# Twelve of fifteen blocks of path comparisons in an alignment kernel: subtraction on GpSimd, one compare on VectorE

## The chip, the cores and the metric

The kernel runs on one core of one Trainium2 chip. The metric is the device time of that core in microseconds (us), the median of several runs. The engines are called PE (TensorE), DVE (VectorE), ACT (ScalarE), POOL (GpSimd) and SP (SyncE, which here only issues DMAs).

## The reference

A batch of 8 sequences of 56 tokens, 128 wide, goes through two gated layers, each an attention-like part and a feed-forward part. The change lies in the first part, an alignment by dynamic time warping of the normalized tokens ("large") with 1500 context rows ("small"):

```python
D = _pairwise_euclidean(small, large)            # 1500 x 56
R = _dtw_cost(D)      # R[i,j] = D[i,j] + min(R[i-1,j], R[i,j-1], R[i-1,j-1])
i_idx, j_idx, valid = _backtrack(R, T_small, T_large)   # argmin of diagonal, up, left, from the far corner
contrib = small[i_idx] * valid[:, None]
expanded = zeros((T_large, d)).at[j_idx].add(contrib)
x = x + tanh(g_xattn[0]) * alignment(ctx_1024, layernorm(x))
```

Then come a product-key memory layer (8 heads, 32 keys, gathers from tables), 16-head attention over the 1500 context rows of each batch (its keys are `ctx @ Wk + bk`), and a layer of 8 experts with the two best taken.

## The kernel before, in words

The cost matrix R is laid out by lanes. Each batch has 16 lanes (partitions); a lane holds 100 context rows at a time (C = 100; 15 stripes of 100 make 1500). The matrix is swept along a skewed front in STEPS = 70 steps of one column each. The R buffer holds one slot of 101 floats per step (SLOT).

**A step** on DVE (the loop `for t in range(STEPS)`, lines 1201 to 1231) is: a minimum of two shifted views of R's slot into `mring` (L1208, TENSOR_TENSOR), a shuffle that hands the last element of a lane to the next (L1209), a wait for the distances of that step, and a scan that adds distances and takes minima (L1213, TENSOR_TENSOR_SCAN), which raises `s_scan`. `mring` has 10 slots, so step t overwrites what step t-10 wrote.

**Blocks.** Steps are grouped in 14 blocks of TB = 5. To walk the path back later, each cell needs a "jump code". For a block k, `jump_inputs(k)` makes two marks per cell on DVE: `left` (L1189: is R's next element smaller than this one) and `never` (L1190: is the new R smaller than the minimum in `mring`). Both are `is_lt` of two float32 tensors, 128x500, with float16 results. It runs at step 9 for block 0, at step 5k+6 for blocks 1 to 12, and at step 68 and after the last step for the halves of the last block. Then PE's `jump_codes(k)` (L1387, L1389, L1391: three matmuls into one PSUM bank) adds them up, and DVE's `jump_targets(k)` (L1198, a scan over 505 elements, from PSUM) turns them into targets, at step 5k+14.

**Beside it.** For each block ACT copies the lane distances (L625, `lane_distances`, one block ahead of use) and works on key pieces of the second layer's attention: 32 pieces of 375 columns, each split in three bfloat16 parts by three ACT copies (L634, L640 twice) between which PE takes the rounded part off (L1370). `KEYS_OF_CHUNK` says how many pieces PE and ACT do in each block: 0, 1, then seven times 3, then five times 2. PE issues `jump_codes(k-2)` in chunk k, after the first key piece of that chunk. In the first 9 steps DVE also makes squared distances of 12 units, `d2_of(u)` (L849, from PSUM), placed by `D2_AT` before steps 1, 3, 5 and 8; units 8, 9 and 10 all stand before step 5. Each one is turned by PE (L1316), goes through a square root on ACT (L611) and is turned back into lane order (L1356). POOL does nothing between 24 us and 125 us.

**After it** come 69 hops back along the path (L1244 on DVE, L1452 on PE), the sums, and the other layers, one behind the other.

SP waits for `s_nv` of all 15 blocks before it loads the folding weights and the rest of the context.

Of the kernel before, what the change touches and what calls it, by code (L numbers as in the profile page):

```python
# [22 lines left out]
def view(ap, dims, offset=0):  # L23

    return bass.AP(tensor=ap.tensor, offset=ap.offset + offset, ap=[list(ap.ap[0])] + dims)


def build_gated_layers(nc, x_T, ctx_T, ctx_nat, g_xattn, g_ffn, weights, fold_w, w_tab, W1, W2, out):
# [5 lines left out]
    C = 100  # L34
# [39 lines left out]
    KPB = NI // KPIECE  # L74
    NKP = NB * KPB
    KBANKS = (4, 5, 6, 7)
    KEYS_OF_CHUNK = [0, 1] + 7 * [3] + 5 * [2]
    KEY_STEPS = [range(sum(KEYS_OF_CHUNK[:k]), sum(KEYS_OF_CHUNK[:k + 1])) for k in range(NTB)]
    assert KPIECE * KPB == NI and KRING == len(KBANKS) and NKP == sum(KEYS_OF_CHUNK)

# [15 lines left out]
    PAIR_BANK = (0, 1, 6)  # L96
    JOBS = [(i, lo, hi) for lo, hi in ((0, CUT), (CUT, TOK)) for i in range(FC)] + [(i, 0, TOK) for i in range(FC, NE * FC)]
    MORE = len(JOBS) - NE * FC
    CODES = [(k * TB, TB) for k in range(NTB - 1)] + [(STEPS - TB, TB - 1), (STEPS - 1, 1)]
    NCODES = len(CODES)  # L100
    TILES = (range(3), range(3, 4))
# [2 lines left out]
    with ExitStack() as ctx:  # L104
# [3 lines left out]
        def sem(name):  # L108
            return ctx.enter_context(nc.semaphore(name))
# [34 lines left out]

        mring = work[:, 0:2 * N_B]
        dts = work[:, 2 * N_B:4 * N_B]
        left = [work[:, 6 * N_B + a * N_B // 2:6 * N_B + (a + 1) * N_B // 2].bitcast(F16) for a in range(2)]
        o_nv = 8 * N_B + KQW
        never = [w.bitcast(F16) for w in (work[:, 7 * N_B + N_B // 2:8 * N_B], work[:, o_nv:o_nv + N_B // 2])]
        assert o_nv + N_B // 2 <= 10 * N_B  # L150
        gate = work[:, 10 * N_B:]
        taken = 0

# [275 lines left out]
        def _(sp):  # L429
# [10 lines left out]
            for n in range(NKP):  # L440
                store_keys(n)
                if n in (4, 10):
                    b = 1 + n // 10
                    sp.wait_ge(s_turn, UN)
                    sp.dma_start(nat[b], ctx_nat[:, b, :, :].rearrange("c s d -> c (s d)")).then_inc(s_nat2[b], 16)
            sp.wait_ge(s_nv, NCODES)
            sp.dma_start(foldw, fold_w[:, :]).then_inc(s_wqT, 16)
            for b in (0, *range(3, NB)):
                if b >= 3:
# [41 lines left out]
        def _(pool):  # L491
# [35 lines left out]
            pool.wait_ge(s_t, 2)  # L527
            done2(nc.gpsimd.tensor_tensor(mk[:, 1:2], mk2[:, :], mk[:, 0:1], ALU.subtract))
            done2(nc.gpsimd.tensor_scalar(mku[:, :], mk2[:, :], -1.0, 1.0, ALU.mult, ALU.add))
            pool.wait_ge(s_dt, NTB)  # L530
            for r in range(STORES):
                pool.wait_ge(s_kd[r], 16 * len(range(r, NKP, STORES)))
# [285 lines left out]
        def _(ve):  # L818
# [24 lines left out]
            def d2_of(u):  # L843

                ve.wait_ge(s_dot, u + 1)
                if u >= D_RING:
                    ve.wait_ge(s_turn, u - D_RING + 1)
                g = u % PAIRS
                nc.vector.tensor_scalar(sd[:, u % D_RING, :], ps[4 + u % 2][:, 0:PIECE], bbc[:, g:g + 1], 0.0,  # L849
                                        ALU.add, ALU.max).then_inc(s_d2, 1)  # L850
# [330 lines left out]

            shift = [LB - 1] + list(range(LB - 1)) + [2 * LB - 1] + list(range(LB, 2 * LB - 1))

            three = lambda a: a.rearrange("p (t c) -> p t c", c=C)

            def jump_inputs(k):

                t, n = CODES[k]
                nc.vector.tensor_tensor(three(left_of(k)), R_slot(t, n, 1, C), R_slot(t, n, 0, C), ALU.is_lt)  # L1189
                nc.vector.tensor_tensor(three(never_of(k)), R_slot(t + 1, n, 0, C),  # L1190
                                        three(mring[:, t % (2 * TB) * C:(t % (2 * TB) + n) * C]), ALU.is_lt
                                        ).then_inc(s_nv, 1)

            def jump_targets(k):

# [2 lines left out]
                nc.vector.tensor_tensor_scan(where[:, t * SLOT:(t + n) * SLOT], gate[:, 0:n * SLOT],  # L1198
                                             ps[3 - k % 2][:, 0:n * SLOT], 0.0, ALU.add, ALU.max).then_inc(s_carry, 1)

            D2_AT = {1: (6,), 3: (7,), 5: (8, 9, 10), 8: (11,)}
            for t in range(STEPS):
                for u in D2_AT.get(t, ()):
                    d2_of(u)
                m = mring[:, (t % (2 * TB)) * C:(t % (2 * TB) + 1) * C]
                if t >= 1:
                    ve.wait_ge(s_scan, t)
                nc.vector.tensor_tensor(m, R_slot(t, 1, 1, C), R_slot(t, 1, 0, C), ALU.min)  # L1208
                link(nc.vector.stream_shuffle(R_slot(t + 1, 1, 0, 1), R_slot(t, 1, C, 1), shift))  # L1209
                if t % DT_STEPS == 0:  # L1210
                    ve.wait_ge(s_dtc, t // DT_STEPS + 1)
                d = dts[:, (t % (2 * DT_STEPS)) * C:(t % (2 * DT_STEPS) + 1) * C]
                nc.vector.tensor_tensor_scan(view(R, [[1, C]], (t + 1) * SLOT + 1), m, d,  # L1213
                                             R[:, (t + 1) * SLOT:(t + 1) * SLOT + 1], ALU.min, ALU.add
                                             ).then_inc(s_scan, 1)
                if t == 2 * TB - 1:
                    ve.wait_ge(s_scan, t + 1)
                    jump_inputs(0)
                    link(nc.vector.tensor_scalar(lane_i[:, :], pidx[:, :], DH, None, ALU.bitwise_and))
                    nc.vector.tensor_scalar(rowc21[:, :], rowc2[:, :], 1.0, None, ALU.add)  # L1220
                    link(nc.vector.tensor_copy(hm[:, 0:1], lane_i[:, :]))
                    link(nc.vector.tensor_scalar(hm[:, 1:2], hm[:, 0:1], 0.0, None, ALU.is_gt))
                    link(nc.vector.tensor_scalar(hm[:, 0:1], hm[:, 1:2], 0.0, None, ALU.is_equal))
                if t % TB == 1 and t >= 2 * TB:
                    jump_inputs(t // TB - 1)
                if t == STEPS - 2:
                    ve.wait_ge(s_scan, t + 1)
                    ve.wait_ge(s_code, NTB - 2)
                    jump_inputs(NTB - 1)
                if t % TB == 4 and t >= 2 * TB:  # L1230
                    jump_targets(t // TB - 2)
            ve.wait_ge(s_scan, STEPS)
            jump_inputs(NTB)
            for k in range(NTB - 2, NCODES):
                jump_targets(k)

# [43 lines left out]
        def _(pe):  # L1280
# [98 lines left out]
                    take_off(n - 1, 1)  # L1379

            def jump_codes(k):
                pe.wait_ge(s_nv, k + 1)
                if k >= 2:
                    pe.wait_ge(s_carry, k - 1)
                bank, n = ps[3 - k % 2], CODES[k][1]
                inner = view(bank, [[SLOT, n], [1, C]], 1)
                nc.tensor.matmul(bank[:, 0:n * SLOT], one16[:, :], steps16[:, 0:n * SLOT], start=True, stop=False,  # L1387
                                 skip_group_check=True)
                nc.tensor.matmul(inner, one16[:, :], left_of(k), start=False, stop=False,  # L1389
                                 skip_group_check=True)  # L1390
                nc.tensor.matmul(inner, never16[:, :], never_of(k), start=False, stop=True,  # L1391
                                 skip_group_check=True).then_inc(s_code, 1)
# [407 lines left out]
```

## Time and profile before

| | |
|---|---|
| median of 3 runs | 517.43 us (517.33 to 517.56) |
| the profiled execution | 516.99 us, of which the span from first to last instruction 515.2 us |
| granted TensorE clock, mean | 0.946 |
| DVE busy | 372.8 us (72%) |
| PE busy | 422.9 us (82%) |
| ACT, POOL busy | 255.2 us (50%), 64.7 us (13%) |
| steps 0 to 69 | scans from 26.4 us to 118.1 us of the span |

A timeline row gives the start in us, the duration in us, the engine, the line of the kernel, the operation, what it writes and reads, partitions x elements with types, and how many instructions are merged in the row. In square brackets stands how long the engine was idle before it and who released it. A DVE instruction may start a little before the one in front has ended, so costs are best taken from start to start.

### The profile page before, as it was taken

Reading aid. Unit: us, or ns where it says so; the run is one execution under the profiler, and the core shown is the slowest. Engines: PE = TensorE matmul, PEld = TensorE weight load, DVE = VectorE, ACT = ScalarE, POOL = GpSimd, SP = SyncE. Lnnn points to the kernel's source line nnn. Section 1 sums busy time; section 2 is a strip of 40 time slices with the busy share of each in tenths; the row PEclk is TensorE's granted clock in tenths of the full one; section 3 lists DMA queues with packets and bytes.
Section 4 is the critical chain, followed back from the end, with each engine's and each line's share of the span. In section 5 each row is a group of like instructions: output and inputs, shape, how many; then the busy total and the mean of one; then the engine's idle time right before and its main releaser. Section 6 shows DMA issues by size and latency. Waiting matters only on the chain.

```text
span 515.2 us, 10127 instructions
## 1 busy us (share of the span) xinstructions
PE 422.9 (82%) x4013; PEld 253.2 (49%) x4013; DVE 372.8 (72%) x979; ACT 255.2 (50%) x442; POOL 64.7 (13%) x99
## 2 busy tenths in 40 slices
PE   8998877677888888200788899999999999989996
PEld 5444433345555574000334456666666666654443
DVE  7659999997666794865686898888888884462222
ACT  4665877553322591100102456665666567655443
POOL 1000000001000001677430000210210210200000
PEclk9999999888999999655789999999999999999999
DMA  8600764334422103893162004383483582000000
GB/s 283 241 0 25 213 198 144 102 125 122 153 60 80 41 3 67 204 240 90 56 135 50 1 1 101 84 180 86 98 180 74 111 269 62 1 1 1 0 1 18
DMA packets 28941, 50.28 MB, mean 98 GB/s; under 512 B 2470, under 2 KB 18622, under 8 KB 28894
## 3 DMA queue, kind: packets, MB, share of 16 engines
q1 hardware_dynamic: 27070, 45.96, 33.0%
q0 software_dynamic: 1536, 3.67, 2.9%
q8 instruction: 32, 0.52, 0.5%
q14 instruction: 15, 0.12, 0.1%
q10 hardware_dynamic: 288, 0.00, 0.0%
HBM read 39.96 MB, written 9.45 MB: 96 GB/s over the span
## 4 chain that ended last, share of the span: by engine, by line
PE 47%; DVE 35%; issue 7%; POOL 6%; ACT 2%; DMA 1%; DVEq 0%
PE banks L1608 7%; PE banks L1584 7%; POOL arena L554 6%; PE banks L1639 5%; DVE arena L1213 5%; PE banks L1681 5%; DVE work L1244 5%; DVE mx L1019 4%; PE banks L1696 4%; DVE arena L1268 2%; PE banks L1452 2%; DVE work L1208 2%; DVE mx L1027 2%; PE banks L1301 2%; PE banks L1323 2%
## 5 line engine op out<-in xcount | busy, mean ns | idle before, releaser
L1019 DVE TENSOR_REDUCE mx<-banks 112x1 f32<-112x500 f32 x168 | 107.1, 675 | 16.4 <-PE banks L1584 16.4
L762 ACT ACTIVATE arena<-banks 128x896 f32<-128x896 f32 x96 | 87.9, 917 | 48.3 <-PE banks L1639 47.7
L1323 PE MATMUL banks<-steps,one 128*128 128x500 f16 (+1 forms) x188 | 53.8, 380 | 32.9 <-DVE hcol L967 32.9
L1608 PE MATMUL banks<-arena 128*32 128x112 f32 (+1 forms) x1536 | 57.1, 265 | 1.5 <-ACT arena L762 0.9
L1584 PE MATMUL banks<-ctxT,arena 96*112 96x500 bf16 x144 | 54.7, 393 | 3.8 <-DVE mx L1019 1.1
L1608 PEld LDWEIGHTS banks<-arena 128*32 128x32 f32 (+1 forms) x1536 | 33.6, 109 | 21.5 <-issue 18.9
L1244 DVE SCALAR_TENSOR_TENSOR work<-twice,banks,arena 128x202 f32<-128x202 f32 x68 | 29.5, 434 | 18.7 <-PE banks L1452 18.7
L1639 PEld LDWEIGHTS banks<-arena,ctxT 99*128 99x128 bf16 (+1 forms) x576 | 37.5, 103 | 10.2 <-issue 2.4
L1323 PEld LDWEIGHTS banks<-steps,one 128*128 128x128 f16 x188 | 19.2, 104 | 47.1 <-issue 37.4
L1639 PE MATMUL banks<-arena,ctxT 99*128 99x112 bf16 (+1 forms) x576 | 41.2, 213 | 0.3 <-issue 0.3
L640 ACT ACTIVATE arena<-banks,wts 128x375 bf16<-128x375 f32 x64 | 33.9, 597 | 7.5 <-PE banks L1370 7.5
L554 POOL DMA_INDIRECT arena<-in_w_tab,idx x32 | 34.3, 1071 | 17.9 <-issue 9.4
L1400 PE MATMUL banks<-wts,ctxT 128*128 128x128 f32 x192 | 34.8, 283 | 0.0
L775 ACT ACTIVATE arena<-banks,wts 128x448 f32<-128x448 f32 (+2 forms) x36 | 21.3, 592 | 25.0 <-PE banks L1681 24.7
L1213 DVE TENSOR_TENSOR_SCAN arena<-work,arena 128x100 f32<-128x100 f32 x70 | 29.8, 426 | 4.3 <-ACT work L625 1.8
L1400 PEld LDWEIGHTS banks<-wts,ctxT 128*128 128x128 f32 x192 | 32.4, 197 | 0.5 <-issue 0.2
L1370 PE MATMUL banks<-arena,minusb 128*128 128x375 bf16 x64 | 19.1, 342 | 15.8 <-ACT arena L634 14.4
L1681 PE MATMUL banks<-xnT,arena 128*128 128x448 f32 (+2 forms) x72 | 31.1, 514 | 0.0
L671 ACT ACTIVATE arena<-banks 128x512 f32<-128x512 f32 (+2 forms) x32 | 14.2, 492 | 33.3 <-PE banks L1400 31.4
L1363 PE MATMUL banks<-ctxT,wts 128*128 128x375 f32 x64 | 27.4, 514 | 0.0
L1584 PEld LDWEIGHTS banks<-ctxT,arena 96*112 96x112 bf16 x144 | 18.1, 128 | 17.5 <-issue 9.5
L1696 PE MATMUL banks<-arena 128*128 128x448 f32 (+2 forms) x64 | 26.5, 496 | 0.0
(269 smaller groups left out, 697.7 us busy)
## 6 DMA issues: line engine op xcount, KB each, us to landing
ctxT<-key_parts SPq DMA_DIRECT2D x36, 375.0 KB, 6.7
key_parts<-arena SPq DMA_DIRECT2D x32, 281.2 KB, 3.1
ctxT<-in_ctx_T SPq DMA_DIRECT2D x12, 500.0 KB, 9.0
arena<-key_parts SPq DMA_DIRECT2D x12, 375.0 KB, 7.8
ctxT<-in_ctx_nat SPq DMA_DIRECT2D x5, 750.0 KB
arena<-in_ctx_nat SPq DMA_DIRECT2D x3, 750.0 KB
arena<-in_L_ffn_W SPq DMA_DIRECT2D x1, 2048.0 KB, 9.7
arena<-in_fold_w SPq DMA_DIRECT2D x1, 768.0 KB, 6.0
```

Of the source, the lines that this page charges most:

```text
L554: nc.gpsimd.indirect_dma_start(out=gath[:, t, h, :], out_offset=None, in_=w_tab[:, :], in_offset=bass.IndirectOffsetOnAxis(ap=idx[:, c:c + ...
L762: nc.scalar.activation(Pt[0:rows, g % 2, :].rearrange("p (a n) -> p a n", a=2), banks[0:rows, 2 + 2 * (g % 2):4 + 2 * (g % 2), 0:HQ // 2], ...
L1019: nc.vector.tensor_reduce(mx3[:, b % 2, u // NPIECE, u % NPIECE:u % NPIECE + 1], ps[k % 2][0:2 * NJ, 0:PIECE], AX_X, ALU.max).then_inc(s_m ...
L1213: nc.vector.tensor_tensor_scan(view(R, [[1, C]], (t + 1) * SLOT + 1), m, d, R[:, (t + 1) * SLOT:(t + 1) * SLOT + 1], ALU.min, ALU.add).the ...
L1244: nc.vector.scalar_tensor_tensor(out=hit_at.rearrange("p (c k) -> p c k", k=2), in0=twice[:, :].rearrange("p (c k) -> p c k", k=2), scalar ...
L1323: nc.tensor.matmul(bank[:, 0:cols], one16[:, :], steps16[:, 0:cols], start=True, stop=True, skip_group_check=True)
L1400: last = nc.tensor.matmul(ps[VALUE_BANKS[n % 6]][0:rows, k * D:(k + 1) * D], ctxT[:, b * NI + c * P:b * NI + c * P + rows], Wv_sb, start=T ...
L1584: nc.tensor.matmul(ps[k % ring][0:2 * NJ, 0:PIECE], QP[0:NPR, u // NPIECE, b, :], KP[b % 3][0:NPR, u // NPIECE, (u % NPIECE) * PIECE:(u % ...
L1608: last = nc.tensor.matmul(ps[6 + b % 2][q:q + 32, o:o + 2 * NJ], vals[0:rows, v0:v0 + 32], Pt[0:rows, g % 2, 2 * t * NJ:2 * (t + 1) * NJ], ...
L1639: last = nc.tensor.matmul(bank[0:rows, o:o + 2 * NJ], KP[b % 3][0:NPR + 3, m, c * P:c * P + rows], QP[0:NPR + 3, m, b, :], start=True, sto ...
L1681: nc.tensor.matmul(ps[5 + j % 2][:, lo:hi], W1s[:, e, c * P:(c + 1) * P], xnT[:, lo:hi], start=True, stop=True, skip_group_check=True).the ...
L1696: nc.tensor.matmul(ps[7 if e % 2 else 0][:, lo:hi], W2s[:, i, :], hT[:, i % 4, lo:hi], start=(c == 0), stop=(c == FC - 1), skip_group_chec ...
```

## The change

It takes the two compares of blocks 0 to 11 off DVE. POOL subtracts instead (two TENSOR_TENSOR of 128x500 elements per block, float32 in, bfloat16 out, both results side by side in a `gaps` buffer), and DVE makes both marks with one TENSOR_SCALAR `is_lt 0` over 1000 bfloat16 elements, float16 out (`signs_of`), after the scan of step 5k+10. POOL starts block k when the scan of step 5k+4 is done. DVE waits for POOL's block before a step that would overwrite `mring` (at steps 10, 15, ...). Blocks 12, 13 and 14 keep the two compares (`moves_of`), at the places they had. The key pieces are dealt out in another order, five small table instructions move from behind step 9 to in between units 8 and 9, and unit 10 moves from before step 5 to before step 6.

```diff
-    KEYS_OF_CHUNK = [0, 1] + 7 * [3] + 5 * [2]
+    KEYS_OF_CHUNK = [0, 1] + [3, 2, 3, 3, 2, 3, 2, 3, 3, 2, 3, 2]
+    SIDE = NTB - 2
-        left = [work[:, 6 * N_B + a * N_B // 2:6 * N_B + (a + 1) * N_B // 2].bitcast(F16) for a in range(2)]
-        never = [w.bitcast(F16) for w in (work[:, 7 * N_B + N_B // 2:8 * N_B], work[:, o_nv:o_nv + N_B // 2])]
+        moves = [work[:, (6 + a) * N_B:(7 + a) * N_B].bitcast(F16) for a in range(2)]
+        left = [m[:, 0:N_B] for m in moves]
+        never = [m[:, N_B:2 * N_B] for m in moves]
+        gaps = [work[:, (4 + a) * N_B:(5 + a) * N_B].bitcast(BF16) for a in range(2)]
@@ SP
-            sp.wait_ge(s_nv, NCODES)
+            sp.wait_ge(s_nv, SIDE)
+            sp.wait_ge(s_nvl, NCODES - SIDE)
@@ POOL
+            for k in range(SIDE):
+                pool.wait_ge(s_scan, CODES[k][0] + TB)
+                if k >= 2:
+                    pool.wait_ge(s_nv, k - 1)
+                t, n = CODES[k]
+                nc.gpsimd.tensor_tensor(three(gaps[k % 2][:, 0:N_B]), R_slot(t, n, 1, C), R_slot(t, n, 0, C), ALU.subtract)
+                nc.gpsimd.tensor_tensor(three(gaps[k % 2][:, N_B:2 * N_B]), R_slot(t + 1, n, 0, C),
+                                        three(mring[:, t % (2 * TB) * C:(t % (2 * TB) + n) * C]), ALU.subtract
+                                        ).then_inc(s_gap, 1)
@@ DVE
-            def jump_inputs(k):
+            def moves_of(k):
...
-                                        ).then_inc(s_nv, 1)
+                                        ).then_inc(s_nvl, 1)
+            def signs_of(k):
+                ve.wait_ge(s_gap, k + 1)
+                if k >= 2:
+                    ve.wait_ge(s_code, k - 1)
+                nc.vector.tensor_scalar(moves[k % 2][:, :], gaps[k % 2][:, :], 0.0, None, ALU.is_lt).then_inc(s_nv, 1)
...
-            D2_AT = {1: (6,), 3: (7,), 5: (8, 9, 10), 8: (11,)}
+            D2_AT = {1: (6,), 3: (7,), 5: (8, 9), 6: (10,), 8: (11,)}
             for t in range(STEPS):
                 for u in D2_AT.get(t, ()):
                     d2_of(u)
+                    if u == 8:
+                        spare_tables()
...
+                if t % TB == 0 and t >= 2 * TB:
+                    ve.wait_ge(s_gap, min(t // TB - 1, SIDE))
...
-                if t == 2 * TB - 1:
-                    ve.wait_ge(s_scan, t + 1)
-                    jump_inputs(0)
...
-                if t % TB == 1 and t >= 2 * TB:
-                    jump_inputs(t // TB - 1)
+                if t % TB == 0 and 2 * TB <= t < (SIDE + 2) * TB:
+                    signs_of(t // TB - 2)
+                if t == SIDE * TB + TB + 1:
+                    ve.wait_ge(s_code, SIDE - 1)
+                    moves_of(SIDE)
@@ PE
-                pe.wait_ge(s_nv, k + 1)
+                pe.wait_ge(s_nv if k < SIDE else s_nvl, k + 1 if k < SIDE else k + 1 - SIDE)
```

## Rows read from the trace of the kernel before

**Rows 1.** The page: the chain that ended last, shares of the span.
```profile
PE 47%; DVE 35%; issue 7%; POOL 6%; ACT 2%; DMA 1%; DVEq 0%
```

**Rows 2.** Windows: length, then PE, PEld, DVE, ACT, POOL busy, clock, DMA share, GB/s.
```profile
50.00:75.00 25.00, 20.30 (x89) 10.38 (x88) 23.88 (x93) 20.14 (x44) 0.00 (x0) 1.00 0.70 214
```

**Rows 3.** Timeline of DVE, one block, from one jump_targets to the next.
```profile
73.97 0.43 DVE L1213 TENSOR_TENSOR_SCAN arena<-work,arena 128x100 f32<-128x100 f32 x1
74.32 1.18 DVE L1198 TENSOR_TENSOR_SCAN arena<-work,banks 128x505 f16<-128x505 f32 x1
75.41 0.24 DVE L1208 TENSOR_TENSOR work<-arena 128x100 f32<-128x100 f32 x1
...
76.22 0.26 DVE L1208 TENSOR_TENSOR work<-arena 128x100 f32<-128x100 f32 x1
...
76.94 0.65 DVE L1189 TENSOR_TENSOR work<-arena 128x500 f16<-128x500 f32 x1
77.51 0.67 DVE L1190 TENSOR_TENSOR work<-arena,work 128x500 f16<-128x500 f32 x1
78.10 0.26 DVE L1208 TENSOR_TENSOR work<-arena 128x100 f32<-128x100 f32 x1
...
78.93 0.27 DVE L1208 TENSOR_TENSOR work<-arena 128x100 f32<-128x100 f32 x1
...
80.49 1.18 DVE L1198 TENSOR_TENSOR_SCAN arena<-work,banks 128x505 f16<-128x505 f32 x1
```

**Rows 4.** Groups by line and form: DVE's shuffle of one column, a cast of 896 elements.
```profile
L1209 DVE STREAM_SHUFFLE arena<-arena 128x1 f32<-128x1 f32 x70 | 10.6, 151 | 0.0
...
L1005 DVE CAST work<-arena 128x896 bf16<-128x896 f32 x1 | 0.6, 628 | 0.0
```

**Rows 5.** Groups by line and form: POOL's TENSOR_TENSOR with two full inputs.
```profile
L585 POOL TENSOR_TENSOR work<-work 128x224 f32<-128x224 f32 x7 | 4.6, 660 | 0.6
...
L590 POOL TENSOR_TENSOR work<-work 128x112 f32<-128x112 f32 x7 | 3.0, 423 | 26.7 <-DVE work L1051 26.7
```

**Rows 6.** Timelines of POOL and of DVE where both run at 261 us.
```profile
261.36 1.09 POOL L565 TENSOR_SCALAR_AFFINE_SELECT work<-work 24x1024 bf16<-24x1024 bf16 x1
...
261.66 0.27 DVE L904 TENSOR_TENSOR xc<-xT,banks 128x112 f32<-128x112 f32 x1 [0.66 <-PE banks L1283]
261.96 0.62 DVE L905 TENSOR_TENSOR xsq<-xc 128x112 f32<-128x112 f32 x1
```

**Rows 7.** The same at 442 us, and POOL's line 591: ns min/median/max.
```profile
441.84 0.57 DVE L1102 SCALAR_TENSOR_TENSOR xT<-xc,gt,xT 128x336 f32<-128x336 f32 x1
...
442.00 0.64 POOL L591 TENSOR_TENSOR work<-work,wts 128x112 f32<-128x112 f32 x1
...
L591 POOL TENSOR_TENSOR work<-work,wts x7: 374/375/640, 329.6 to 442.0; 128x112 f32<-128x112 f32 x7
```

**Rows 8.** Timelines of DVE, ACT and PE around steps 5 to 10.
```profile
34.16 0.74 DVE L849 TENSOR_SCALAR arena<-banks,bbc 128x500 f32<-128x500 f32 x1 [1.77 <-PE banks L1305]
37.23 0.74 DVE L849 TENSOR_SCALAR arena<-banks,bbc 128x500 f32<-128x500 f32 x1 [2.34 <-PE banks L1305]
...
43.73 0.15 DVE L1219 TENSOR_SCALAR lane_i<-pidx 128x1 int32<-128x1 int32 x1
...
44.56 0.26 DVE L1208 TENSOR_TENSOR work<-arena 128x100 f32<-128x100 f32 x1
...
44.93 0.42 DVE L1213 TENSOR_TENSOR_SCAN arena<-work,arena 128x100 f32<-128x100 f32 x1
...
41.03 0.75 PE L1316 MATMUL banks<-ident,arena 128*100 128x128 f32 x5 [0.65 <-DVE arena L849]
...
43.56 0.59 ACT L625 ACTIVATE work<-banks 128x500 f32<-128x500 f32 x1 [1.09 <-PE banks L1356]
```

**Rows 9.** Timelines of PE and ACT in a block with three key pieces.
```profile
76.23 0.38 PE L1387 MATMUL banks<-steps,one 128*128 128x505 f16 x1
...
80.67 0.59 ACT L625 ACTIVATE work<-banks 128x500 f32<-128x500 f32 x1 [1.40 <-DVE arena L1213]
```

More of the change, by code:

```diff
@@ L146, in build_gated_layers @@
         dts = work[:, 2 * N_B:4 * N_B]
-        left = [work[:, 6 * N_B + a * N_B // 2:6 * N_B + (a + 1) * N_B // 2].bitcast(F16) for a in range(2)]
-        o_nv = 8 * N_B + KQW
-        never = [w.bitcast(F16) for w in (work[:, 7 * N_B + N_B // 2:8 * N_B], work[:, o_nv:o_nv + N_B // 2])]
-        assert o_nv + N_B // 2 <= 10 * N_B
+        moves = [work[:, (6 + a) * N_B:(7 + a) * N_B].bitcast(F16) for a in range(2)]
+        left = [m[:, 0:N_B] for m in moves]
+        never = [m[:, N_B:2 * N_B] for m in moves]
+        gaps = [work[:, (4 + a) * N_B:(5 + a) * N_B].bitcast(BF16) for a in range(2)]
         gate = work[:, 10 * N_B:]
@@ L328, in build_gated_layers @@
         s_scan = sem("column_scanned")
+        s_gap = sem("moves_compared")
+        s_nvl = sem("last_not_left_marks_ready")
         s_nv = sem("rows_not_left_ready")
@@ L422, in left_of @@
             return left_last[:, :] if k == NCODES - 1 else left[k % 2][:, 0:CODES[k][1] * C]
+        three = lambda a: a.rearrange("p (t c) -> p t c", c=C)
         R_slot = lambda k, n, lo, cnt: view(R[:, :], [[SLOT, n], [1, cnt]], k * SLOT + lo)
@@ L1182, in _ @@
             shift = [LB - 1] + list(range(LB - 1)) + [2 * LB - 1] + list(range(LB, 2 * LB - 1))
-            three = lambda a: a.rearrange("p (t c) -> p t c", c=C)
-            def jump_inputs(k):
+            def moves_of(k):
                 t, n = CODES[k]
@@ L1199, in jump_targets, with spare_tables @@
                                              ps[3 - k % 2][:, 0:n * SLOT], 0.0, ALU.add, ALU.max).then_inc(s_carry, 1)
-            D2_AT = {1: (6,), 3: (7,), 5: (8, 9, 10), 8: (11,)}
+            def spare_tables():
+                link(nc.vector.tensor_scalar(lane_i[:, :], pidx[:, :], DH, None, ALU.bitwise_and))
+                nc.vector.tensor_scalar(rowc21[:, :], rowc2[:, :], 1.0, None, ALU.add)
+                link(nc.vector.tensor_copy(hm[:, 0:1], lane_i[:, :]))
+                link(nc.vector.tensor_scalar(hm[:, 1:2], hm[:, 0:1], 0.0, None, ALU.is_gt))
+                link(nc.vector.tensor_scalar(hm[:, 0:1], hm[:, 1:2], 0.0, None, ALU.is_equal))
+            D2_AT = {1: (6,), 3: (7,), 5: (8, 9), 6: (10,), 8: (11,)}
             for t in range(STEPS):
@@ L1215, in _ @@
                                              ).then_inc(s_scan, 1)
-                if t == 2 * TB - 1:
-                    ve.wait_ge(s_scan, t + 1)
-                    jump_inputs(0)
[L1219 to L1223, printed above, removed]
-                if t % TB == 1 and t >= 2 * TB:
-                    jump_inputs(t // TB - 1)
+                if t % TB == 0 and 2 * TB <= t < (SIDE + 2) * TB:
[3 more added lines that the diff above has]
+                    moves_of(SIDE)
                 if t == STEPS - 2:
@@ L1228, in _ @@
                     ve.wait_ge(s_code, NTB - 2)
-                    jump_inputs(NTB - 1)
+                    moves_of(NTB - 1)
                 if t % TB == 4 and t >= 2 * TB:
@@ L1232, in _ @@
             ve.wait_ge(s_scan, STEPS)
-            jump_inputs(NTB)
+            moves_of(NTB)
             for k in range(NTB - 2, NCODES):
```

## The prediction

> **What bounds the kernel now.** I read the chain first [rows 1]: PE and DVE share it, so the kernel is a row of stages, each with its own limit, and a change counts only in its stage. The change lies in steps 0 to 69, before 122 us. The windows say what limits there [rows 2]: between 50 and 75 us DVE is busy for 23.88 of 25.00 us, ACT for 20.14, POOL not at all. The timeline of one block [rows 3] says the same in detail: DVE runs from one jump_targets (74.32) to the next (80.49), 6.17 us, without an idle gap that another engine ended. After step 69 the hops follow at once, and they wait for DVE's last targets. So a microsecond that DVE gains or loses in steps 10 to 69 is one of the whole kernel, as long as DVE stays the limit.
>
> **One block taken apart** [rows 3]. A plain step takes 0.83 us (78.10 to 78.93; over several steps 0.84). The step with the two compares takes 1.88 us (76.22 to 78.10), so the pair costs 1.04. The step scan at 73.97 is over at 74.40; call this T. The next minimum would start 0.03 later, and starts at 75.41 because of jump_targets: 0.98. Sum: 5 x 0.84 + 1.04 + 0.98 = 6.2, which is the 6.17 seen.
>
> **Removed.** Blocks 0 to 11 lose the pair: 1.04 us each.
>
> **Added on DVE: the compare with zero.** No row shows a single-source instruction with 16-bit input in SBUF. A cast of 896 float32 elements takes 0.63 us, about 0.15 of it fixed (a shuffle of one column takes 0.15) [rows 4]. At that rate per element, 1000 elements take 0.15 + 0.53 = 0.68; at that rate per byte read (2000 bytes against 3584) 0.15 + 0.27 = 0.42. At no rate can it be under 0.15. The cast reads and writes nearly as many bytes as fit, so I take 0.42. It starts 0.08 before the scan in front has ended (80.49 against 80.57 [rows 3]) and the next minimum then follows 0.08 before its end, where a minimum otherwise starts 0.03 after the scan: 0.42 - 0.08 - 0.08 - 0.03 = 0.23 net. The ends are 0 and 0.50.
> The Trainium skill ("VectorE: DVE Perf Modes", the perf-mode tier table) gives 693 ns for 2048 bfloat16 elements of a tensor_scalar, four per cycle; an estimate from it is 0.41 us here. The sum would stay as it is.
>
> **Moved to POOL: two subtractions a block.** POOL's TENSOR_TENSOR with two full inputs takes 0.423 us for 112 elements and 0.660 for 224 [rows 5], so 2.12 ns an element and 0.19 fixed: 1.25 us for 500. Two take 2.5 us in a block of about 6, so POOL is no limit by its own time. The results are used five steps later, and `mring` is overwritten five steps later, so DVE's new wait for POOL costs 0.
>
> **What it costs on DVE is another thing.** While POOL ran an instruction from 261.36 to 262.45, DVE's L904, which has one input in PSUM, took its plain 0.27 us. L905, the same size with both inputs in SBUF, started at 261.96 and took 0.62: it was held until POOL had ended, and was done 0.13 later [rows 6]. At 442 us it is the other way round: DVE's L1102 ran to 442.41, and POOL's L591 took 0.64 where its median is 0.375, done 0.23 after DVE [rows 7]. So a DVE instruction with two SBUF inputs and a POOL instruction that reads SBUF don't run together here; the second one waits for the whole of the first.
> The Trainium skill ("SBUF — State Buffer", who interferes with whom) has this as a rule: the shared port pair is an exclusive lock, and the second to issue is blocked for the whole instruction. Both places in this trace agree with it. By a reader who took the ports as free, the sum would come out faster; that is the first rival below.
>
> DVE's minimum (L1208) and step scan (L1213) both have two SBUF inputs; jump_targets has one in PSUM and is free of this. One block then runs so. POOL starts at T + 0.08 and ends its first subtraction at T + 1.33. DVE is in jump_targets until then; its minimum is issued at T + 1.01 and held to T + 1.33, done at T + 1.45. The shuffle has one input. The second subtraction reads on from T + 1.45 for 1.06 us, to T + 2.52. The scan is issued at T + 1.56, held, and done some 0.25 after POOL, at T + 2.77. In the trace it is done 0.03 before the minimum at 76.22 [rows 3], T + 1.79. Cost: 0.98 us a block. If POOL keeps the ports between its two instructions, the minimum is held as well, to T + 2.6, and the scan ends at T + 3.16: 1.37. Rows 6 show DVE let in at POOL's end, but POOL's next one waited for a semaphore there. I take 1.1, nearer to the row. The ends are 0 (no collision) and 1.7 (POOL at 1.4 us each, and keeping the ports). When the compare with zero comes, POOL is done.
>
> So a block changes by -1.04 + 0.23 + 1.10 = +0.29. There are ten such (the steps 15 to 64): **+2.9 us**.
>
> **Front.** Unit 9 waits 1.77 us and unit 10 waits 2.34 [rows 8]. The five table instructions (43.73 to 44.56, 0.83) move into the first wait, step 5 (0.84) into the second; both are hidden, and if POOL's first block holds some of them, the wait still covers it. Units 11, its turn and its lane distances follow PE, not DVE alone: PE waited 0.65 for DVE at 41.03, so L625 at 43.56 comes 0.6 earlier, done at 43.55, and the scan of step 10 (before: 44.93 to 45.35) can't start sooner. But block 1's subtractions start at 42.2, are held by one minimum, and end at 44.6; the scan then ends at 44.85. So 0.5 is won there; block 1's pair goes (1.04), one compare with zero comes (0.23): **-1.3 us**. Without a collision it is 2.2.
>
> **End.** Block 11's compare stands at step 65, its pair is already counted: **+0.2**. Blocks 12 to 14 are as before.
>
> **Key pieces: 0.** In a three-piece block ACT idles 1.40 us before the next lane distances [rows 9]. PE gets to the jump codes at T + 1.83 (76.23) and will now wait for the compare, done at T + 3.1, so 1.3 later, with one more key piece behind it. That fits into the 1.40 and the longer block, and a two-piece block gives slack back; the distances are made a block ahead. POOL's and SP's queues hold nothing that is due before step 69.
>
> **Sum:** 2.9 - 1.3 + 0.2 = +1.8 us. The profiled execution took 516.99 us, 0.44 below the median; it would be 518.8, and the median 517.43 + 1.8 = **519.2 us**. In this case's own bounds (0.8 to 1.4 for the collision, 0.23 to 0.5 for the compare) it lies between 515.7 and 524.
>
> **Rivals.**
> *The ports don't collide for these instructions* (POOL's reads yield, or its lock is short). Then a block changes by -0.81: 10 x -0.81 - 2.2 + 0.2 = -10.1, about 507.3 us. Rows 6 and 7 speak against it; they show two events, one of another POOL operation. It decides the sign: below 0.81 us of collision a block the ten blocks gain, and half a collision gives 512. Chance 0.20.
> *The compare takes one or two elements a cycle, not four.* 0.68 us, 0.50 net: 12 x 0.27 = 3.2 more, 522.4 us. That the change doesn't do what it says would be this. Chance 0.08.
> *PE and ACT become the limit* in the seven three-piece blocks, since PE's jump codes wait for the compare. If the compare ends later than T + 3.1, ACT's slack is gone; 0.3 us in seven blocks is 2 more, 521 us. Against it: slack from one block carries to the next. Chance 0.06.
>
> **Chances.** About 0.2% (1.03 us) is what a measurement of this kernel can tell from no change. My forecast's case has 0.66: with +1.8 in its middle and bounds on both sides of zero, 0.38 slower, 0.18 within, 0.10 faster. Rival one is 0.20 faster. The other two give 0.12 slower, of which 0.02 within. Together: faster 0.30, same 0.20, slower 0.50. The range reaches from 510 (half of the first rival's ground) to 524.
>
> **What would show it.** In the changed trace: POOL's subtractions near 1.25 us; the step scan or minimum right behind jump_targets taking 1 us or more where it took 0.43 and 0.26, and ending just behind a POOL instruction; the compare at 0.42 us; a block at about 6.5 us from one jump_targets to the next, against 6.17. The forecast is wrong if those two stay at 0.43 and 0.26 (then blocks are near 5.4 us), if the compare is near 0.7, or if DVE shows idle time before jump_targets that PE ended.

## The result, and the profile after

The changed kernel takes 514.16 us in the median of 7 runs (513.17 to 515.97), the kernel before 517.46 on the same chip; the ratio is 0.994, 95% interval 0.9921 to 0.9959. That is 3.3 us faster. One of the seven runs of the kernel before took 678.99 us and is left out of the ratio; the other six took 516.38 to 517.68. Forecast was 519.2, slower by 1.8, with 0.30 for faster. The profiled execution took 514.87 us, with a span of 513.1.

The page after, its chain [rows 1]; then the windows [rows 2]:

```profile
PE 47%; DVE 31%; issue 10%; POOL 7%; ACT 2%; DMA 2%; DVEq 0%; POOLq 0%
```
```profile
50.00:75.00 25.00, 19.04 (x84) 9.68 (x82) 23.88 (x89) 19.36 (x41) 9.60 (x9) 1.00 0.64 189
```

DVE is busy for the same 23.88 of 25 us, but with fewer instructions. Part of that "busy" is now waiting inside an instruction. The timeline of DVE shows it, one block from jump_targets (now L1219) to jump_targets [rows 3]; L1240 is the minimum, L1245 the step scan, L1213 the compare with zero:

```profile
72.26 0.42 DVE L1245 TENSOR_TENSOR_SCAN arena<-work,arena 128x100 f32<-128x100 f32 x1
72.60 1.18 DVE L1219 TENSOR_TENSOR_SCAN arena<-work,banks 128x505 f16<-128x505 f32 x1
73.70 0.23 DVE L1240 TENSOR_TENSOR work<-arena 128x100 f32<-128x100 f32 x1
...
74.05 1.11 DVE L1245 TENSOR_TENSOR_SCAN arena<-work,arena 128x100 f32<-128x100 f32 x1
75.08 0.39 DVE L1213 TENSOR_SCALAR work<-work 128x1000 f16<-128x1000 bf16 x1
75.39 0.25 DVE L1240 TENSOR_TENSOR work<-arena 128x100 f32<-128x100 f32 x1
...
78.59 1.18 DVE L1219 TENSOR_TENSOR_SCAN arena<-work,banks 128x505 f16<-128x505 f32 x1
```

The timeline of POOL in the same stretch, and its two lines grouped over all twelve blocks (compare [rows 5]):

```profile
72.76 1.02 POOL L541 TENSOR_TENSOR work<-arena 128x500 bf16<-128x500 f32 x1 [3.83 <-DVE arena L1245]
73.74 1.19 POOL L542 TENSOR_TENSOR work<-arena,work 128x500 bf16<-128x500 f32 x1
```
```profile
L542 POOL TENSOR_TENSOR work<-arena,work 128x500 bf16<-128x500 f32 x12 | 14.4, 1200 | 0.0
L541 POOL TENSOR_TENSOR work<-arena 128x500 bf16<-128x500 f32 x12 | 12.3, 1025 | 54.5 <-DVE arena L1245 54.5
```

The step scan behind jump_targets takes 1.11 us instead of 0.43 and ends at 75.16, 0.23 behind POOL's second subtraction (74.93). A block takes 5.99 us (72.60 to 78.59) where it took 6.17. Eleven scans out of 70 are longer than 0.45 us: ten of 1.10 to 1.15, and that of step 10 with 0.77.

The front, in the timelines of DVE and ACT around steps 5 to 10 [rows 8] (L864 is units 9 and 10, L640 the lane distances):

```profile
34.80 0.74 DVE L864 TENSOR_SCALAR arena<-banks,bbc 128x500 f32<-128x500 f32 x1 [1.13 <-PE banks L1332]
37.56 0.42 DVE L1245 TENSOR_TENSOR_SCAN arena<-work,arena 128x100 f32<-128x100 f32 x1 [1.77 <-ACT work L640]
37.90 0.71 DVE L864 TENSOR_SCALAR arena<-banks,bbc 128x500 f32<-128x500 f32 x1
...
44.33 0.77 DVE L1245 TENSOR_TENSOR_SCAN arena<-work,arena 128x100 f32<-128x100 f32 x1 [1.35 <-ACT work L640]
```
```profile
43.65 0.59 ACT L640 ACTIVATE work<-banks 128x500 f32<-128x500 f32 x1 [1.10 <-PE banks L1383]
```

Where the time went, from the ends of the step scans in both traces (this execution began its steps 0.6 us later than the other, so stretches are compared, not times):

| stretch | before | after | difference | forecast |
|---|---|---|---|---|
| scan 4 to scan 14 | 18.32 | 16.62 | -1.70 | -1.3 |
| scan 14 to 64, ten blocks | 61.66 | 60.16 | -1.50 | +2.9 |
| scan 64 to 69 | 7.14 | 7.32 | +0.18 | +0.2 |
| sum | 87.12 | 84.10 | -3.02 | +1.8 |

The sum of -3.0 is the measured -3.3 within what runs differ by. Behind the last step the two traces are alike: the first hop starts 3.72 us after the last scan before, 3.71 after.

### The profile page after: what moved, and what is told of

Its sections match the earlier page's. It is cut to its first block, busy times and chain, and to the rows that moved or that the text cites. A ratio compares the mean times of both kernels' runs of the same rounds, so it can differ in the third digit from the quotient of the medians.

```text
span 513.1 us, 10171 instructions
## 1 busy us (share of the span) xinstructions
PE 422.1 (82%) x4013; PEld 252.1 (49%) x4013; DVE 369.7 (72%) x967; ACT 255.5 (50%) x442; POOL 91.3 (18%) x123
## 4 chain that ended last, share of the span: by engine, by line
PE 47%; DVE 31%; issue 10%; POOL 7%; ACT 2%; DMA 2%; DVEq 0%; POOLq 0%
PE banks L1635 7%; PE banks L1611 7%; POOL arena L569 7%; PE banks L1666 5%; PE banks L1708 5%; DVE work L1271 5%; DVE mx L1034 5%; PE banks L1723 4%; DVE arena L1245 4%; DVE arena L1295 2%; PE banks L1328 2%; DVE mx L1042 2%; PE banks L1479 2%; DVE work L1240 2%; PE banks L1332 2%
## 5 line engine op out<-in xcount | busy, mean ns | idle before, releaser
L1245 DVE TENSOR_TENSOR_SCAN arena<-work,arena 128x100 f32<-128x100 f32 x70 | 37.2, 531 | 7.3 <-ACT work L640 5.0
L1427 PE MATMUL banks<-wts,ctxT 128*128 128x128 f32 x192 | 33.2, 273 | 0.1
L1427 PEld LDWEIGHTS banks<-wts,ctxT 128*128 128x128 f32 x192 | 30.5, 186 | 0.6 <-ACT arena L686 0.3
L595 POOL TENSOR_TENSOR work<-arena,mk 128x448 f32<-128x448 f32 x7 | 6.5, 932 | 129.9 <-ACT arena L753 129.9
```

The costliest lines, as they stand in the source:

```text
L1427: last = nc.tensor.matmul(ps[VALUE_BANKS[n % 6]][0:rows, k * D:(k + 1) * D], ctxT[:, b * NI + c * P:b * NI + c * P + rows], Wv_sb, start=T ...
```

## The experiments

All are timed beside the kernel before on the same chip, 4 to 10 runs each but for the two of POOL's rates; the chip differs from experiment to experiment, so the ratios compare better than the times. "Block" is the distance of the ends of scans 14, 19, ... in the profiled execution.

### POOL writes, but does not read

```diff
+        spare = [work[:, (8 + a) * N_B:(9 + a) * N_B].bitcast(BF16) for a in range(2)]
...
-                nc.gpsimd.tensor_tensor(three(gaps[k % 2][:, 0:N_B]), R_slot(t, n, 1, C), ...)
-                nc.gpsimd.tensor_tensor(three(gaps[k % 2][:, N_B:2 * N_B]), ...).then_inc(s_gap, 1)
+                nc.gpsimd.memset(spare[k % 2], 0.0)                 # 1000 bfloat16, an unused place
+                nc.gpsimd.memset(gaps[k % 2][:, :], 0.0).then_inc(s_gap, 1)
```

> From the changed kernel; POOL's two subtractions a block become two memsets of 1000 bfloat16 elements each (about 0.9 us each by the memsets in the trace), so POOL works as long but reads nothing. The compare with zero then sees zeros, so the jump codes carry no path. Theory A (a DVE instruction with two SBUF inputs and a POOL instruction that reads SBUF exclude each other): no step scan is longer than 0.43 us, a block goes from 6.0 to about 5.3 us, the kernel to about 507 us. Theory B (any POOL work beside DVE holds it, by writes or by the queue): the scans behind jump_targets stay near 1.1 us, blocks near 6.0, the kernel near 514. Theory C (PE and ACT are the next limit close below): scans at 0.43, but DVE idle in the blocks and blocks over 5.5 us.

This kernel leaves the differences out, so the path that it follows means nothing; it makes the same steps, compares and hops. Measured: 507.33 us, ratio 0.9812 (0.9789 to 0.9835), blocks 5.34 to 5.35. The timelines of DVE and POOL:

```profile
76.00 0.23 DVE L1239 TENSOR_TENSOR work<-arena 128x100 f32<-128x100 f32 x1
...
76.35 0.43 DVE L1244 TENSOR_TENSOR_SCAN arena<-work,arena 128x100 f32<-128x100 f32 x1
76.69 0.43 DVE L1212 TENSOR_SCALAR work<-work 128x1000 f16<-128x1000 bf16 x1
```
```profile
75.92 0.93 POOL L543 MEMSET work<- 128x1000 bf16 x1
```

The scan at 76.35 runs beside POOL's memset (75.92 to 76.85) at its plain 0.43. So POOL's reads hold the two-input instructions, not its work as such, and the 0.67 us a block that this run gives back (6.01 to 5.34) is the price of the collision. Theory A holds, B falls. C did not show from scan 19 on; the two stretches before took 5.69 and 5.65. In the first of them step 10 waits for its distances, in the second DVE waits 0.22 for jump codes from PE. 507.3 is also what the first rival named, the case without a collision.

### The collision alone

```diff
@@ POOL, in the kernel before; jump_inputs unchanged
+            for k in range(SIDE):
+                pool.wait_ge(s_scan, CODES[k][0] + TB)
+                nc.gpsimd.tensor_tensor(...)
+                nc.gpsimd.tensor_tensor(...).then_inc(s_gap, 1)
@@ DVE
+                if t % TB == 0 and t >= 2 * TB:
+                    ve.wait_ge(s_gap, min(t // TB - 1, SIDE))
```

> From the kernel before; POOL makes the same two subtractions at the same points beside it, and nobody uses them; the float32 compares stay on DVE. This is the collision alone. Theory A: the step scan behind jump_targets grows from 0.43 to about 1.1 us, a block from 6.17 to 6.86, ten of them and the front together about 7.5 us, so about 525 us. Theory B' (the long scan of the changed kernel comes from the new order of waits, not from the ports): under 1 us more than before.

Measured: 527.06 us, ratio 1.0192 (1.0159 to 1.0225), blocks 6.83 to 6.89. DVE and POOL:

```profile
46.38 0.93 DVE L1231 TENSOR_SCALAR rowc<-rowc 100x15 f32<-100x15 f32 x1
...
81.77 1.11 DVE L1224 TENSOR_TENSOR_SCAN arena<-work,arena 128x100 f32<-128x100 f32 x1
```
```profile
45.71 1.57 POOL L538 TENSOR_TENSOR work<-arena,work 128x500 bf16<-128x500 f32 x1
...
81.46 1.20 POOL L538 TENSOR_TENSOR work<-arena,work 128x500 bf16<-128x500 f32 x1
```

The same scan grows by the same 0.69, a block from 6.17 to 6.86. The whole costs 9.9 us, not 7.5: the block of steps 10 to 14 takes 8.81 instead of 7.22, since POOL there meets the compares of block 0 (the second took 1.49 for 0.67) and the table instructions. One of these, with one float32 input of 15 columns, took 0.93 (0.17 in the changed kernel) and ended 0.03 behind POOL's second subtraction. From scan 4 to scan 69 that makes 8.6 us; the other 1.3 lie outside the steps, and no run here says why.

### POOL one step later

```diff
-                pool.wait_ge(s_scan, CODES[k][0] + TB)
+                pool.wait_ge(s_scan, CODES[k][0] + TB + 1)
```

> From the changed kernel; POOL starts each block one step later, after the scan of step 5k+5, so that jump_targets no longer runs beside its first subtraction. Theory A: both subtractions now meet only instructions with two SBUF inputs (and the compare with zero); about 1.0 us more is held a block, blocks near 7.0 us, the kernel near 524 us. If jump_targets gives no cover, blocks stay at 6.0 us and the kernel at 514.

Measured: 524.17 us, ratio 1.0141 (1.0115 to 1.0167), blocks 6.81 to 6.87. DVE and POOL:

```profile
86.12 1.08 DVE L1240 TENSOR_TENSOR work<-arena 128x100 f32<-128x100 f32 x1
...
87.31 1.15 DVE L1245 TENSOR_TENSOR_SCAN arena<-work,arena 128x100 f32<-128x100 f32 x1
```
```profile
85.97 1.11 POOL L541 TENSOR_TENSOR work<-arena 128x500 bf16<-128x500 f32 x1 [4.59 <-DVE arena L1245]
87.05 1.20 POOL L542 TENSOR_TENSOR work<-arena,work 128x500 bf16<-128x500 f32 x1
```

Now each of the two subtractions holds one instruction of DVE: 0.82 for the minimum (1.08 less 0.26) and 0.7 for the scan. Between them DVE was let in: the minimum ends at 87.20, 0.12 behind the end of the first subtraction (87.08), and the second one, already started at 87.05, takes 1.20. So POOL does not keep DVE out from one instruction to the next. That jump_targets covers the first subtraction is worth 0.83 us a block, 10 us in all; the place of POOL's start decides the sign of this change.

### What a subtraction costs on POOL

```diff
+            for _ in range(2):
+                for n in (112, 224, 336, 448):
+                    tried_one(xsq[:, 0:n], A0(0, n), A0(200, n))                          # inputs 0 and 200
+                tried_one(grid(xsq[:, :], 4, 56, 56), grid(wts[:, :], 4, 56, 112), grid(wts[:, 56:], 4, 56, 112))
+                tried_one(h16[:, 0:448], A0(0, 448), A0(200, 448))                        # h16: bfloat16 out
...
+                tried_one(grid(h16, 5, 100, 100), grid(wts[:, 1:], 5, 100, 101), grid(wts[:, :], 5, 100, 101))
+                tried_one(xsq[:, :], A0(0, 448), wts[:, 0:1].broadcast_to([P, 448]))
```

> From the changed kernel; 20 more POOL subtractions in a stretch of the attention where POOL is idle and DVE reads only PSUM, on scratch, each of the ten forms twice. It prices the term that the forecast had at 1.25 us and the trace has at 1.02. Theory A: 0.25 us fixed and 1.54 ns an element whatever the output type, so 112, 224, 336, 448 elements give 0.42, 0.60, 0.77, 0.94 us, and only the 4x56 form with stride 112 costs 0.66. Rival: the bfloat16 output is what is cheap, so float32 at 448 gives 1.14 and bfloat16 0.93.

These instructions stand in a stretch where POOL is otherwise idle, and each of the two kernels that hold them ran once (515.24 and 523.59 us); they are read for the durations alone. Measured, first round (the second agrees within 0.02): float32 out, both inputs plain rows 200 elements apart: 0.42, 0.66, 0.91 and 1.13 us for 112, 224, 336 and 448 elements. Four rows of 56, the inputs 56 apart: 0.66. bfloat16 out: 0.66, 1.13 and 1.26 for 224, 448 and 500 elements. Five rows of 100 at step 101, the inputs 1 apart: 1.01. One input a single repeated element, 448: 0.93. Two lines of POOL's timeline, the plain row of 500 and the five rows of 100:

```profile
298.76 1.26 POOL L593 TENSOR_TENSOR xsq<-wts 128x500 bf16<-128x500 f32 x1
...
300.83 1.01 POOL L593 TENSOR_TENSOR xsq<-wts 128x500 bf16<-128x500 f32 x1
```

Neither theory holds. The output type changes nothing (448 elements: 1.13 both ways), and the forecast's rate of 2.12 ns an element is right for plain rows. Yet the form of the kernel costs a fifth less.

```diff
+            for a, b in ((0, 200), (0, 201), (1, 201), (0, 1), (0, 0), (0, 101)):            # plain rows of 500
+                tried_one(grid(a, 1, 500, 500), grid(b, 1, 500, 500))
+            for a, b, s in ((0, 200, 100), (0, 1, 100), (1, 0, 101), (0, 0, 101), (0, 101, 101), (0, 101, 102), (0, 192, 101)):
+                tried_one(grid(a, 5, 100, s), grid(b, 5, 100, s), 5, 100)                     # 5 rows of 100 at step s
+            tried_one(grid(0, 1, 500, 500), grid(4, 1, 500, 500))
+            tried_one(grid(0, 1, 500, 500), grid(8, 1, 500, 500))
```

> From the changed kernel; 15 more POOL subtractions of 500 elements, bfloat16 out, on scratch where POOL is idle: plain rows at several starts, 5 rows of 100 at steps 100, 101 and 102. Before it, plain rows of 500 (starts 0 and 200) took 1.25 us and 5 rows of 100 at step 101 (starts 1 and 0) took 1.02. Theory P (how the starts of the two inputs stand to each other sets the rate): the pairs 0 and 1, 0 and 201, 0 and 101 take 1.02 in either shape, 0 and 200 take 1.25. Theory Q (short rows are faster): all forms of 5 rows take 1.02 and all plain ones 1.25.

Measured, in this order: 1.24, 1.07, 1.25, 1.02, 1.02, 1.07; then 1.25, 1.02, 1.02, 1.02, 1.06, 1.06, 1.25; then 1.02 and 1.25. Four of them, with the inputs 200, 1, 4 and 8 elements apart:

```profile
295.77 1.24 POOL L593 TENSOR_TENSOR xsq<-wts 128x500 bf16<-128x500 f32 x1 [33.10 <-DVE mx L1052]
...
299.56 1.02 POOL L593 TENSOR_TENSOR xsq<-wts 128x500 bf16<-128x500 f32 x1
...
311.15 1.02 POOL L593 TENSOR_TENSOR xsq<-wts 128x500 bf16<-128x500 f32 x1
...
312.25 1.25 POOL L593 TENSOR_TENSOR xsq<-wts 128x500 bf16<-128x500 f32 x1
```

Theory P holds, but for 0.05 at two of its distances, and Q falls: rows and steps don't matter, the distance between the two inputs does. Distances 0, 1 and 4 gave 1.02, 101 and 201 gave 1.06 to 1.07, and 8, 192 and 200 gave 1.25. In the kernel before, the two instructions that I priced by have their inputs 56 and 112 elements apart [rows 5], which are multiples of 8 like the slow ones here, and they cost what plain rows 200 apart cost (0.66 for 224 elements, 0.42 for 112). The kernel's first subtraction has them 1 apart. The fast distances were not tried at 112 or 224 elements.

### One subtraction only

```diff
@@ POOL
-                nc.gpsimd.tensor_tensor(three(gaps[k % 2][:, 0:N_B]), R_slot(t, n, 1, C), R_slot(t, n, 0, C), ALU.subtract)
@@ DVE, signs_of
-                nc.vector.tensor_scalar(moves[k % 2][:, :], gaps[k % 2][:, :], 0.0, None, ALU.is_lt).then_inc(s_nv, 1)
+                t, n = CODES[k]
+                nc.vector.tensor_tensor(three(left_of(k)), R_slot(t, n, 1, C), R_slot(t, n, 0, C), ALU.is_lt)
+                nc.vector.tensor_scalar(never[k % 2], gaps[k % 2][:, N_B:2 * N_B], 0.0, None, ALU.is_lt).then_inc(s_nv, 1)
```

> From the changed kernel; for blocks 0 to 11 POOL makes only the second subtraction (against the minimum), as its first and only one, and DVE makes the other mark itself with a float32 is_lt of 500 elements ahead of a compare with zero of 500 elements. Theory A: the one subtraction of about 1.0 us lies wholly beside jump_targets, so no scan is held (0.69 us a block back) and DVE pays about 0.57 for the float32 mark less 0.13 for the shorter compare. Blocks go from 6.0 to about 5.8 us, the kernel from 514.2 to about 511.8 us. If the collision were not what the second subtraction costs, this would only add 0.44 us a block: about 519 us.

Measured: 514.01 us, ratio 0.9926 (0.9907 to 0.9945), which can't be told from the changed kernel. Blocks 5.85 to 5.91. DVE and POOL:

```profile
73.07 0.32 DVE L1242 TENSOR_TENSOR work<-arena 128x100 f32<-128x100 f32 x1
...
73.50 0.43 DVE L1247 TENSOR_TENSOR_SCAN arena<-work,arena 128x100 f32<-128x100 f32 x1
73.84 0.65 DVE L1213 TENSOR_TENSOR work<-arena 128x500 f16<-128x500 f32 x1
74.42 0.28 DVE L1214 TENSOR_SCALAR work<-work 128x500 f16<-128x500 bf16 x1
```
```profile
72.14 1.13 POOL L541 TENSOR_TENSOR work<-arena,work 128x500 bf16<-128x500 f32 x1 [4.72 <-DVE arena L1247]
```

No scan is held, as expected. But this subtraction (R against the minimum) takes 1.13 to 1.18 us in the blocks (1.23 for the first of them) with no other subtraction before it, not 1.02, and so holds the minimum by 0.1. The block gains 0.13 instead of 0.25, and the last block loses 0.46, since block 11's float32 mark now also stands in it (7.78 against 7.32). The expectation of 511.8 us had left out both.

### Parts put back: the key deal and the front

```diff
-    KEYS_OF_CHUNK = [0, 1] + [3, 2, 3, 3, 2, 3, 2, 3, 3, 2, 3, 2]
+    KEYS_OF_CHUNK = [0, 1] + 7 * [3] + 5 * [2]
```

> From the changed kernel; only the deal of the key pieces is put back (seven times 3, then five times 2). Theory A (DVE is the limit, the deal is worth next to nothing): 514 to 515 us, early blocks at 6.0 or 6.1. Rival (the deal is what gained): about 517 us, with DVE idle in front of jump_targets in the blocks of three pieces.

Measured: 514.72 us, ratio 0.9938 (0.9923 to 0.9954). In its trace scan 4 to scan 69 takes 84.10 us, the same as in the changed kernel. The deal is worth nothing in this stage.

```diff
-            D2_AT = {1: (6,), 3: (7,), 5: (8, 9), 6: (10,), 8: (11,)}
+            D2_AT = {1: (6,), 3: (7,), 5: (8, 9, 10), 8: (11,)}
-                    if u == 8:
-                        spare_tables()
+                if t == 2 * TB - 1:
+                    spare_tables()
```

> From the changed kernel; only unit 10 and the five table instructions are put back where they were (before step 5, behind step 9). Theory A: step 10 waits for lane distances and for POOL anyway, so of the 1.67 us moved only about 0.5 comes back: 514.7 us. If the whole of it counts: 515.8 us.

Measured: 515.35 us, ratio 0.9954 (0.9937 to 0.9971). In the trace, scan 4 to scan 9 takes 11.09 us against 10.60, and all later stretches agree within 0.03: 0.5 us, as theory A has it. The medians differ by 1.2, but the intervals of the two ratios overlap.

### The type of the differences

```diff
-        moves = [work[:, (6 + a) * N_B:(7 + a) * N_B].bitcast(F16) for a in range(2)]
+        moves = [work[:, (8 + a) * N_B:(9 + a) * N_B].bitcast(F16) for a in range(2)]
...
-        gaps = [work[:, (4 + a) * N_B:(5 + a) * N_B].bitcast(BF16) for a in range(2)]
+        gaps = [work[:, (4 + 2 * a) * N_B:(6 + 2 * a) * N_B] for a in range(2)]      # float32
```

> From the changed kernel; POOL writes float32 differences, and DVE's compare reads 1000 float32 elements instead of bfloat16. Theory A: the compare goes from 0.39 to about 0.68 us (the rate of the float32 cast), 0.28 a block for twelve blocks, POOL's subtractions stay at 1.02 us: about 517.5 us. If the type makes POOL's instruction cheap, they grow towards 1.25 as well and a block loses 0.3 more: about 520 us.

Measured: 517.39 us, ratio 0.9995 (0.9981 to 1.0009), blocks 6.25 to 6.30. DVE's scan is as before, the compare grows:

```profile
74.95 1.11 DVE L1245 TENSOR_TENSOR_SCAN arena<-work,arena 128x100 f32<-128x100 f32 x1
75.98 0.65 DVE L1213 TENSOR_SCALAR work<-work 128x1000 f16<-128x1000 f32 x1
```

POOL's first subtraction stays at 1.02 us, so the type does not make it cheap. Bfloat16 is worth 0.26 us of DVE in each of twelve blocks, 3.1 us, which is about as much as the change gains: with float32 differences it is a draw with the kernel before.

### Distances read from PSUM

```diff
@@ DVE, the step
-                    ve.wait_ge(s_dtc, t // DT_STEPS + 1)
-                d = dts[:, (t % (2 * DT_STEPS)) * C:(t % (2 * DT_STEPS) + 1) * C]
+                    ve.wait_ge(s_dt, t // DT_STEPS + 1)
+                d = ps[t // DT_STEPS % 2][:, t % DT_STEPS * C:(t % DT_STEPS + 1) * C]
@@ PE, lane_columns (and no lane_distances on ACT)
-                    pe.wait_ge(s_dtc, q - 1)
+                    pe.wait_ge(s_scan, DT_STEPS * (q - 1))
@@ PE, the end: four value tiles wait for scan 65, eight stand behind jump_codes(NTB - 2) and scan 70
```

> From the changed kernel; the step scan reads the distances from the PSUM bank in which PE has turned them, and ACT's copy to SBUF is left out. PE now waits where ACT waited, and four value tiles come later, behind the last step. Theory A (it is the second SBUF input that a POOL read holds up): the scan behind jump_targets takes its plain 0.43 us while POOL's second subtraction runs, and the hold moves to the compare with zero, which reads SBUF alone but came out fast: 0.39 grows to about 0.9, blocks near 5.9 us. If any DVE read of SBUF were held, the scan would stay at 1.1.

Measured: 513.25 us, ratio 0.9894 (0.986 to 0.9929), blocks 5.72 to 5.76. DVE and POOL:

```profile
72.18 0.42 DVE L1241 TENSOR_TENSOR_SCAN arena<-work,arena,banks 128x100 f32<-128x100 f32 x1
72.52 0.83 DVE L1209 TENSOR_SCALAR work<-work 128x1000 f16<-128x1000 bf16 x1
...
117.46 1.34 DVE L1215 TENSOR_TENSOR_SCAN arena<-work,banks 128x404 f16<-128x404 f32 x2 [2.34 <-PE banks L1414]
```
```profile
71.88 1.19 POOL L542 TENSOR_TENSOR work<-arena,work 128x500 bf16<-128x500 f32 x1
```

The scan with one input in PSUM runs at 0.42 beside POOL's read, and the hold moves to the compare, which reads only one tensor but is held all the same (0.83 for 0.39). The block gains 0.27, and the step scan is no slower from PSUM. The last row shows what this version loses: behind the last step DVE waits 2.34 us for jump codes that stand behind value tiles on PE.

### A faster version

```diff
-    VALUE_BANKS = (0, 1, 4, 5, 6, 7)
-    EARLY_VALUES = 16
+    VALUE_BANKS = (0, 4, 1, 5, 6, 7)
+    EARLY_VALUES = 14
@@ PE, the end
+            jump_codes(NTB - 2)      # then value tiles 4 to 7
+            jump_codes(NTB - 1)      # then scan 70, tiles 8 to 10
+            jump_codes(NTB)          # then tiles 11 to 13
```

> From distances_in_psum; the end of the stage is put in order: the value tiles that have to wait for a bank now stand behind the jump codes that DVE waits for (the second group in bank 4, the third in bank 1, two early tiles fewer). DVE idled 2.34 us there, behind the last step. Theory A: that comes back, blocks stay at 5.74 us, the kernel goes from 513.2 to about 511 us. If the gain of the blocks is lost elsewhere: 513.

Measured: 511.4 us, ratio 0.9895 (0.9873 to 0.9918), blocks 5.73 to 5.76. The first hop follows the last scan after 3.71 us again, where it was 6.26. The ratios of this version and the one before it (0.9894) can't be told apart, so this gain too rests on the traces.

```diff
-                if t % TB == 0 and 2 * TB <= t < (SIDE + 2) * TB:
+                if t % TB == 1 and 2 * TB <= t < (SIDE + 2) * TB:
                     signs_of(t // TB - 2)
```

> From psum_tail; the compare with zero moves one step later, behind the scan of step 5k+11. Theory A: POOL's second subtraction has then ended when the compare comes (0.39 again), but it holds the minimum of that step, which reads twice from SBUF, by about 0.3 us where it held the compare by 0.43. Blocks about 5.6 us, the kernel about 509.7 us. Rival: jump codes that start 0.8 us later let PE and ACT fall behind in three-piece blocks, and the gain is not seen.

Measured: 510.55 us, ratio 0.988 (0.9857 to 0.9903), blocks 5.58 to 5.62. DVE:

```profile
77.24 0.58 DVE L1236 TENSOR_TENSOR work<-arena 128x100 f32<-128x100 f32 x1
...
78.27 0.40 DVE L1209 TENSOR_SCALAR work<-work 128x1000 f16<-128x1000 bf16 x1
```

The minimum is held by 0.32 and the compare is plain: 0.14 a block less. From scan 4 to scan 69 that gives 1.44 us, but in this trace the second and third hop wait 0.68 and 0.99 us for PE, where a hop of the version before waits 0.27; 509.7 us was expected. This is the fastest version here, 6 to 7 us under the kernel before; the intervals of the last two overlap, so the last step rests on the trace.

## Why the prediction was wrong

- **What bounds the stage**: right. DVE has no gap that another engine ended in the blocks, and the stage's 3.0 us are the kernel's gain.
- **The collision**: right in kind and place. The scan right behind jump_targets is held and ends 0.23 behind POOL, jump_targets covers the first subtraction, and the minimum gets in between the two.
- **The step that failed is the size of that term.** The prediction put "0.19 fixed: 1.25 us for 500", and from it 0.98 us of hold, raised to 1.10. The subtractions took 1.02 and 1.20, and the hold was 0.69. The rate came from two rows whose inputs stand 112 and 56 elements apart; by the two runs of POOL's rates such distances are of the slow kind, and the kernel's first subtraction, 1 apart, is of the fast (1.02). Put the two measured durations into the prediction's own steps, and they come out right: the first subtraction ends at T + 1.10, the minimum is done at T + 1.22, the second subtraction reads on for 1.20 less 0.19, to T + 2.23, and the scan is done 0.25 later, at T + 2.48, where the trace has 75.16 - 72.68 = 2.48. The 1.02 is explained by the distance; why the second one takes 1.20 is only measured.
- The 0.12 that was added for the case that POOL keeps the ports was wrong too. It doesn't, as the timeline of the run with POOL one step later shows. Without the 0.12 the forecast would have been 1.2 lower, +0.6 instead of +1.8, and still not faster: the rate is the larger part (0.29 of the 0.41 a block).
- **The compare with zero**: 0.42 forecast, 0.39 measured; net 0.20 a block against 0.23 (75.39 less 75.16, less the 0.03 that always follows a scan).
- With both, a block changes by -1.04 + 0.20 + 0.69 = -0.15, and ten of them by the -1.5 of the table. The prediction had named the line itself, 0.81 us of hold a block: the true value lies 0.12 under it, the forecast 0.29 over it. Its lower bound of 0.8 for this term was too near: it allowed for little error in POOL's rate, and the measured 0.69 lies outside it. That 514.16 lies in the range from 510 to 524 is no merit of this term, for the range was widened downwards for the first rival. The case's own bounds don't come out of its terms either: 0.8 and 1.4 for the collision, with 0.23 and 0.5 for the compare, give 516.2 and 525.4, not 515.7 and 524, and half a collision gives about 513, not 512.
- **The front**: -1.3 forecast, -1.70 measured. The lane distances did come 0.5 earlier relative to step 4, and the scan of step 10 was held, but only for 0.35, since POOL was done at 44.88. It is the same term again. Putting the two moves back costs 0.5.
- **Key pieces at 0, end at +0.2**: right (84.10 us of steps with either deal; +0.18).
- The rival without a collision was priced at 507.3; taking POOL's reads away gave 507.33. That it agrees to 0.03 is luck: against the kernel before on its own chip that run gained 9.9, the rival 10.1.

## What to carry to other kernels

Work given to GpSimd that reads SBUF was paid for here where VectorE ran an instruction with two SBUF inputs, or the compare with zero, and this can be most of the work's own length (with POOL one step later, 1.5 of 2.3 us); so start it where VectorE runs something that reads PSUM (here jump_targets: 0.83 us a block), or give VectorE one of its inputs from PSUM (0.27 us a block more). When the sign of a forecast hangs on one duration, price it by a row with the same layout of operands, and if there is none, keep its bound wide. The gain of a change can sit in a detail: here the 16-bit type of the differences is worth as much as the whole.

## What the hardware showed that I had not expected

- The time of a GpSimd subtraction of 500 elements depends on how far its two inputs are apart in a partition: 1.02 us at 0, 1 and 4 elements of float32, 1.06 to 1.07 at 101 and 201, 1.25 at 8, 192 and 200. Output type and row shape changed nothing. Why is open, and other distances were not tried. R against the minimum takes 1.13 to 1.23; there the rows of the inputs step by 101 and 100, so the distance changes from row to row, which no run tried by itself.
- The compare on VectorE, with one 16-bit input in SBUF, is held by a GpSimd read just like a two-input instruction (0.83 us for 0.39). The Trainium skill ("SBUF — State Buffer", who interferes with whom) has it so for the fast modes of a tensor_scalar, and this run agrees. The table instruction with one float32 input of 15 columns was held as well (0.93 for 0.17, beside POOL in the kernel before).
- A step scan with its distances in PSUM is as quick as with them in SBUF (0.42 us both).
